# Pairing attention heads anew and sending the first pair's row of maxima of batch 0 by itself

## The chip, the cores and the metric

One Trainium2 chip, one core. The metric is the device time of the kernel in microseconds, the median of several executions.

## The reference, cut to what matters

Eight sequences of 512 token ids pass a token embedding (a row of a table times a 64 x 64 matrix chosen by the token's rule), one attention layer and one mixture-of-experts layer, each behind a layernorm and added to the residual. Only the attention concerns the change:

```python
def _L0_attn_ref(x, Q, K, VO):                        # x (8, 512, 64), Q and K (8, 32, 64), VO (8, 64, 64)
    q = jnp.einsum('btd,hrd->bhtr', x, Q)
    k = jnp.einsum('bud,hrd->bhur', x, K)
    scores = jnp.einsum('bhtr,bhur->bhtu', q, k) / sqrt(d)
    attn = jax.nn.softmax(scores, axis=-1)
    ctx = jnp.einsum('bhtu,bud->bhtd', attn, x)
    return jnp.einsum('bhtd,hde->bte', ctx, VO)
h = _L0_tok_ref(...)
h = h + _L0_attn_ref(_layernorm(h), ...)
h = h + _L0_ffn_ref(_layernorm(h), ...)
```

## The kernel before, in words

**The token stage.** Tokens are scattered into an order by rule in DRAM, in two halves: batches 0 and 1, then batches 2 to 7. Groups of 512 rows are loaded (e_in), transposed on TensorE (turn, L1146, "rT"), copied by ScalarE to eT (L705), multiplied by their rule's matrix (apply, L1155, "rule"), copied by VectorE to y_out (L1022), stored to y_sorted and at last gathered back by GpSimd into hbuf (bring, L551). The first half has 15 groups and is done before the attention begins. The second half has 19 groups. They run as 20 slots in stage 0, in the steps that R_AT gives; a slot is the transposition of one group and the rule of the one before. For them GpSimd issues loads (L413) and stores (L418), and behind the last store the gathers of batches 2 and 3.

**Stages and steps.** From there every engine walks the same loop: a stage b for each batch (from -2), with 16 steps k in each. The order on each engine is written out by hand. In step k of stage b TensorE does: two score tiles for the exponentials, transposed (L1278, keys times queries), one step ahead of their use; up to two score tiles for the maxima of the next batch (s_units, L1303), one before and one after the values; the values (L1319, four matmuls); and what aux_at lists for that step (the lists order, slot and ring give each of these a place in banks 6, 7 and 4). ScalarE takes the exponentials (L684) and copies, VectorE the maxima (L1016), layernorms, the low parts of split numbers and copies. SP's queue is written as one list of DMAs and waits.

**Scores and their maxima.** Queries and keys of a batch come from four projections (proj, L1207 and L1208: two for Q, two for K, four heads of 32 rows in each), split into a high part (qk_h, ScalarE, L753) and a low part (qk_l, VectorE, L1083). stack(b, g) then sends, by DMA, for each row group g of 32 the heads g and 4 + g to three bands of rows of qs and ks: six DMAs of 128 KB a group, 24 a batch (L465 for qs and L468 for ks on SP; for batch 0 the keys' twelve are on ScalarE, L676). Head slots 2g and 2g+1 receive them side by side, so a row of 4 KB stays whole. Each maximum of 128 query rows of a head over its 512 keys is one unit: a matmul and a reduction, 32 a batch. A unit of batch 0 below 16 (first_pair, L1261) reads qk_h and qk_l directly, two heads at a time with three matmuls each, since the stack is still on its way. After 16 units TensorE transposes the maxima ("mt", L1239), ScalarE negates them into negm (L758), and SP sends them as row 96 of qs (max_row, L474), where the exponentials' score tiles pick them up: the matmul of 97 rows subtracts them. Its semaphore is m_in, and the score tiles of head pairs 0 and 1 wait for the first half's row.

**Around the change, before.** The 32 units of batch 0 are in steps (-1, 4) to (0, 3), two a step (LEAD is 12). The transposition mt of its first half is at (-1, 11), behind unit 15. The first two score tiles for the exponentials stand at the head of step (-1, 15), behind unit 21. The rule row of the second half (L1122) follows them. Units 0 to 15 use banks 3 and 4 or 0 and 1 in turn; units 26 to 35 bank 3 alone, as bank 4 serves the rule groups then. The slots are three in step (0, 1), three in (0, 2), eight in (0, 3), three in (0, 4) and three in (0, 5); of a step's slots one stands before the values and the rest behind the other work. xT(1) (L1203) and two projections of batch 1 are in (0, 2), two in (0, 3). The layernorm of batch 1 is in (0, 0) and (0, 1), that of batch 2 begins at (0, 10), that of batch 3 at (0, 15).

Of the kernel before, what the change touches and what calls it, by code (L numbers as in the profile page):

```python
# [24 lines left out]
def packed_weights(Q, K, VO, Wg, bg, gbias, W1, b1, W2, b2):  # L25

    H, R, D = Q.shape
    NE, _, HID = W1.shape
    half = [m.reshape(2, H // 2 * R, D) for m in (Q, K)]
    wqk = np.concatenate([h.transpose(2, 0, 1).reshape(D, -1) for h in half], axis=1)  # L30
    w1 = W1.transpose(1, 0, 2).reshape(D, -1)
    wqk, w1, wg = (np.concatenate([m, m], axis=0) for m in (wqk, w1, Wg))
    vo = np.zeros((2, D, H // 2, 2, D), np.float32)
    row0 = np.zeros((2, D, H // 2, D), np.float32)
    for hh in range(2):
        vo[hh, :, :, hh, :] = VO[hh * (H // 2):(hh + 1) * (H // 2)].transpose(1, 0, 2)
        row0[hh] = VO[hh * (H // 2):(hh + 1) * (H // 2), 0][None]
    w2 = W2.transpose(1, 0, 2).reshape(HID, -1)
    b2p = b2.reshape(NE // 2, 2, D).transpose(1, 2, 0).reshape(2 * D, -1)
    rows = [np.broadcast_to(v[None, :], (128, NE)) for v in (bg, gbias)]  # L40
    stay = [vo.reshape(128, -1), row0.reshape(128, -1), w2, b1.T, b2p, wg] + rows
    return np.ascontiguousarray(np.concatenate(stay + [wqk, w1], axis=1).astype(np.float32))


def lm_tower_kernel(nc, ids_in, table, rules, weights, consts, out, dims):
# [6 lines left out]
    J = T // 128  # L52
# [26 lines left out]
    with ctx:  # L79
# [93 lines left out]
        with ExitStack() as part:  # L173
# [7 lines left out]
            scattered_0 scattered_1 eT_ps eT_ok y_ps y_ok xn_ready xa_ready w_h ones_ok w_ok xT_ps x_hi xs_ready  # L181
            xT2_ps x2_hi xs2_ready proj_ps qk_hi qk_lo ks_one s_ps mx_done mt_ps negm_ready m_in
            st_ps exp_done pv_done ctx_copied srow_in rt_ps rsum_ready vo_ps vo_used h1_ready
# [61 lines left out]

        R_AT = [(0, 1 + g // 3) for g in range(6)] + [(0, 3)] * 8 + [(0, 4 + g // 3) for g in range(6)]

# [9 lines left out]
        def aux_at(b, k):  # L257
# [44 lines left out]
        in_four = max(n for n in range(r0, r1 + 1) if place_of[n] == 4)  # L302
        ONE, TWO = 26, 36

# [16 lines left out]
        def emptied(eng, n):  # L321
# [4 lines left out]
            if kind == "rule":  # L326
                eng.wait_ge(S["y_ok"], b + 1)
            if kind == "mt":
                eng.wait_ge(S["negm_ready"], 2 * b + i + 1)
# [105 lines left out]
        def _(sp):  # L435
# [22 lines left out]
            def stack(b, g):  # L458

                if g == 0:  # L460
                    sp.wait_ge(S["qk_lo"], 4 * b + 4)
                if b >= 2:
                    sp.wait_ge(S["exp_done"], 32 * (b - 2) + 8 * (g + 1))
                for s, src in enumerate((qk_h, qk_l, qk_h)):
                    sp.dma_start(qs[32 * s:32 * s + 32, b % 2, 2 * g:2 * g + 2, :].bitcast(F32),  # L465
                                 src[32 * g:32 * g + 32, 0:2, :].bitcast(F32)).then_inc(S[f"stack_{g}"], 16)
                for s, src in enumerate((qk_h, qk_h, qk_l) if b else ()):
                    sp.dma_start(ks[32 * s:32 * s + 32, b % 2, 2 * g:2 * g + 2, :].bitcast(F32),  # L468
                                 src[32 * g:32 * g + 32, 2:4, :].bitcast(F32)).then_inc(S[f"stack_{g}"], 16)

            def max_row(b, half):

                sp.wait_ge(S["negm_ready"], 2 * b + half + 1)
                sp.dma_start(qs[96:97, b % 2, 4 * half:4 * half + 4, :].rearrange("o h (t n) -> o (h t) n", n=128).bitcast(F32),  # L474
                             negm[:, half, :].bitcast(F32)).then_inc(S["m_in"], 16)
                sp.wait_ge(S["m_in"], 32 * b + 16 * half + 16)
# [6 lines left out]
            for b in range(-2, B):  # L483
# [163 lines left out]
        def _(act):  # L647
# [22 lines left out]
            for b in range(-2, B + 1):  # L670
                for k in range(16):
                    if (b, k) == (-2, PROJ[3] + 1):
                        act.wait_ge(S["qk_lo"], 4)
                        for g in range(4):
                            for s, src in enumerate((qk_h, qk_h, qk_l)):
                                act.dma_start(ks[32 * s:32 * s + 32, 0, 2 * g:2 * g + 2, :].bitcast(F32),  # L676
                                              src[32 * g:32 * g + 32, 2:4, :].bitcast(F32)).then_inc(S[f"stack_{g}"], 16)
# [14 lines left out]
                    for n_, a in enumerate(aux_at(b, k) + [("", 0, 0)]):  # L692
# [61 lines left out]
                        if kind == "mt":  # L754
                            act.wait_ge(S["mt_ps"], 2 * ab + i + 1)
                            if ab >= 1:
# [8 lines left out]
        def _(dve):  # L765
# [224 lines left out]
            for b in range(-2, B + 1):  # L990
# [3 lines left out]
                for k in range(16):  # L994
# [15 lines left out]
                    for nb, u in s_units(b, k):  # L1010
                        n = 32 * nb + u
                        dve.wait_ge(S["s_ps"], n + 1)
                        if nb >= 1 and u % 16 == 0:
                            dve.wait_ge(S["mt_ps"], 2 * nb - 1 + u // 16)
                        at_ = u % 16 if n >= 16 else n % 2 * 8 + n // 2
                        V.tensor_reduce(mx[:, u // 16, at_:at_ + 1], score_bank(n)[:], AX.X, ALU.max).then_inc(S["mx_done"], 1)  # L1016
# [86 lines left out]
        def _(pe):  # L1103
# [82 lines left out]
            def aux(a):  # L1186
# [42 lines left out]
                if kind == "back":  # L1229
# [4 lines left out]
                    for p in range(NE // 2):  # L1234
                        last = nc.tensor.transpose(out_[:, p * 128:(p + 1) * 128], hid_of(f)[:, 2 * p, j * 128:(j + 1) * 128], ident)
                    last.then_inc(S["bk_ps"], 1)
                if kind == "mt":
                    pe.wait_ge(S["mx_done"], 32 * b + 16 * (i + 1))
# [27 lines left out]
            for b in range(-2, B + 1):  # L1266
                for k in range(16):
                    step = 16 * b + k + 1
                    for u in (2 * step, 2 * step + 1):
                        if 0 <= u < 32 * B:  # L1270
                            ub, pair, ut, th = scored(u)
                            pe.wait_ge(S["m_in"], 32 * ub + 16 * (pair // 2 + 1))
                            if u >= NST:
# [14 lines left out]
                    def score_tile():  # L1288
# [9 lines left out]
                        h, tt = u // J, u % J  # L1298
                        pe.wait_ge(S[f"stack_{h // 2}"], 96 * (nb + 1))
                        if n == TWO:  # L1300
# [8 lines left out]
                    if 0 <= b < B:  # L1309
# [58 lines left out]
```

## Time and profile before

| | us |
|---|---|
| median of 3 runs | 592.49 (586.88 to 597.73) |
| the profiled execution's own time | 592.44 |
| its span | 590.4 |
| PE busy | 498.6 (84%) |
| VectorE busy | 417.8 (71%) |
| ScalarE busy | 280.3 (47%) |
| GpSimd busy | 228.2 (39%) |

PE, DVE, ACT, POOL and SP are TensorE, VectorE, ScalarE, GpSimd and SyncE. A timeline has one line for one or several like instructions in a row: start and length in us, engine, line of the kernel, operation, tile written and tiles read, how many, and in brackets how long the engine had stood before and what released it. ACTq and SPq are the issues of DMAs by these engines.

### The profile page before, as it was taken

Reading aid. Unit: us, or ns where it says so; the run is one execution under the profiler, and the core shown is the slowest. Engines: PE = TensorE matmul, PEld = TensorE weight load, DVE = VectorE, ACT = ScalarE, POOL = GpSimd, SP = SyncE. Lnnn points to the kernel's source line nnn. Section 1 sums busy time; section 2 is a strip of 40 time slices with the busy share of each in tenths; the row PEclk is TensorE's granted clock in tenths of the full one; section 3 lists DMA queues with packets and bytes.
Section 4 is the critical chain, followed back from the end, with each engine's and each line's share of the span. In section 5 each row is a group of like instructions: output and inputs, shape, how many; then the busy total and the mean of one; then the engine's idle time right before and its main releaser. Section 6 shows DMA issues by size and latency. Waiting matters only on the chain.

```text
span 590.4 us, 9478 instructions
## 1 busy us (share of the span) xinstructions
PE 498.6 (84%) x2764; PEld 272.0 (46%) x2764; DVE 417.8 (71%) x1008; ACT 280.3 (47%) x562; POOL 228.2 (39%) x375
## 2 busy tenths in 40 slices
PE   0169337876889899999999999999999899999984
PEld 0037314354534344455445534544454455576663
DVE  6644688753376869889698869968865975755477
ACT  0205110245444454565645565555556455556773
POOL 5787376624262002502551253133122513281542
PEclk9997855589897899999999999999999999999988
DMA  8826218426710724404402340422045000000000
GB/s 232 317 81 192 80 26 184 121 73 194 210 45 12 161 56 107 119 2 108 116 5 59 76 100 2 108 64 54 3 107 118 1 2 12 2 11 1 11 2 18
DMA packets 21791, 47.05 MB, mean 80 GB/s; under 512 B 6248, under 2 KB 11576, under 8 KB 21680
## 3 DMA queue, kind: packets, MB, share of 16 engines
q1 hardware_dynamic: 15408, 32.23, 22.3%
q0 software_dynamic: 4752, 8.20, 4.9%
q10 hardware_dynamic: 1584, 6.03, 3.2%
q8 instruction: 25, 0.41, 0.3%
q14 instruction: 22, 0.18, 0.1%
HBM read 9.97 MB, written 11.01 MB: 36 GB/s over the span
## 4 chain that ended last, share of the span: by engine, by line
PE 59%; DVE 19%; issue 7%; POOL 6%; ACT 3%; DMA 3%; SPq 3%; DVEq 0%; ACTq 0%; POOLq 0%
PE bank L1319 14%; PE bank L1303 10%; PE bank L1278 7%; DVE mx L1016 4%; PE bank L1226 4%; PE bank L1248 4%; PE bank L1155 4%; POOL ctxT L535 3%; PE bank L1220 2%; PE bank L1146 2%; PE bank L1221 2%; PE bank L1330 2%; DVE r_sb L1078 1%; SPq L465 1%; POOL emb_sorted L543 1%
## 5 line engine op out<-in xcount | busy, mean ns | idle before, releaser
L1016 DVE TENSOR_REDUCE mx<-bank 128x1 f32<-128x512 f32 x256 | 170.7, 687 | 59.1 <-PE bank L1303 54.5
L604 POOL TENSOR_TENSOR r_sb<-r_sb 128x256 f32<-128x256 f32 x174 | 90.6, 521 | 244.7 <-DVE r_sb L1096 164.1
L684 ACT ACTIVATE prob<-bank 128x512 f32<-128x512 f32 x256 | 138.8, 596 | 71.5 <-PE bank L1278 59.0
L1319 PE MATMUL bank<-prob,xa 128*64 128x512 f32 x448 | 124.1, 633 | 0.0
L1303 PE MATMUL bank<-ks,qs 96*128 96x512 f32 x240 | 112.2, 471 | 12.1 <-DVE mx L1016 12.0
L1303 PEld LDWEIGHTS bank<-ks,qs 96*128 96x128 f32 x240 | 46.5, 195 | 121.4 <-issue 103.9
L1278 PE MATMUL bank<-qs,ks 97*128 97x512 f32 x224 | 78.5, 433 | 0.0
L747 ACT ACTIVATE r_sb<-bank,stay 128x512 f32<-128x512 f32 x56 | 37.1, 687 | 44.8 <-PE bank L1221 44.6
L1278 PEld LDWEIGHTS bank<-qs,ks 97*128 97x128 f32 x224 | 39.5, 198 | 15.4 <-issue 10.5
L1319 PEld LDWEIGHTS bank<-prob,xa 128*64 128x64 f32 x448 | 22.6, 137 | 37.5 <-issue 35.2
L551 POOL DMA_INDIRECT hbuf<-y_sorted,pos x32 | 31.3, 978 | 20.2 <-DMA y_sorted<-y_out 11.5
L535 POOL DMA_INDIRECT ctxT<-in_table,ids x32 | 32.4, 1011 | 13.5 <-issue 9.3
L543 POOL DMA_INDIRECT emb_sorted<-ctxT,pos x32 | 32.4, 1011 | 12.8 <-issue 9.6
L1248 PE MATMUL bank<-stay,ctxT 128*128 128x128 f32 x256 | 33.7, 276 | 0.1
L1248 PEld LDWEIGHTS bank<-stay,ctxT 128*128 128x128 f32 x256 | 32.4, 191 | 2.2 <-ACT negm L758 0.4
L753 ACT CAST qk_h<-bank 128x512 fp32r<-128x512 f32 x32 | 18.4, 588 | 26.8 <-PE bank L1208 24.1
L1220 PE MATMUL bank<-xs,w_h 128*128 128x512 f32 (+1 forms) x72 | 29.8, 419 | 0.0
L1226 PE MATMUL bank<-r_sb,stay 128*64 128x512 f32 x112 | 27.8, 606 | 1.6 <-ACT r_sb L747 1.6
L1155 PE MATMUL bank<-r_sb,eT 128*64 128x64 f32 (+1 forms) x544 | 26.6, 249 | 2.5 <-DVE y_out L1022 0.9
L1083 DVE TENSOR_TENSOR qk_l<-bank,qk_h 128x512 fp32r<-128x512 f32 x32 | 21.7, 688 | 9.9 <-ACT qk_h L753 9.6
L1096 DVE TENSOR_TENSOR r_sb<-bank,rsum 128x512 f32<-128x512 f32 x30 | 20.7, 691 | 10.4 <-PE bank L1248 7.4
L1221 PE MATMUL bank<-xs,w_l 128*128 128x512 f32 (+1 forms) x72 | 27.0, 380 | 0.0
(173 smaller groups left out, 676.1 us busy)
## 6 DMA issues: line engine op xcount, KB each, us to landing
qs<-qk_h SPq DMA_DIRECT2D x64, 128.0 KB, 2.5
ks<-qk_h SPq DMA_DIRECT2D x56, 128.0 KB, 2.5
qs<-qk_l SPq DMA_DIRECT2D x32, 128.0 KB, 2.5
ks<-qk_l SPq DMA_DIRECT2D x28, 128.0 KB, 2.5
emb_sorted<-front ACTq DMA_DIRECT2D x4, 608.0 KB, 10.3
y_sorted<-y_out POOLq DMA_DIRECT2D x19, 128.0 KB, 3.4
e_in<-emb_sorted POOLq DMA_DIRECT2D x9, 256.0 KB, 4.1
emb_sorted<-front ACTq DMA_DIRECT2D x3, 640.0 KB, 9.3
```

The costliest lines, as they stand in the source:

```text
L535: nc.gpsimd.indirect_dma_start(etok[:, c, :], None, table, bass.IndirectOffsetOnAxis(ap=ids[:, 1, c:c + 1], axis=0)).then_inc(e_got[c // Q ...
L604: nc.gpsimd.tensor_tensor(a[:, at:at + width], src[:, 0:width], src[:, width:2 * width], ALU.add).then_inc(S["pool_chain"], 1)
L684: nc.scalar.activation(prob[:, step % NPROB, u % 2, :], bank[u % NST][:], ACT.Exp, scale=SC).then_inc(S["exp_done"], 1)
L1016: V.tensor_reduce(mx[:, u // 16, at_:at_ + 1], score_bank(n)[:], AX.X, ALU.max).then_inc(S["mx_done"], 1)
L1155: last = M(out_[half * TS:(half + 1) * TS, c * D:(c + 1) * D], eT[:, g % 2, col:col + TS], r_sb[:, at_:at_ + D] if isinstance(at_, int) el ...
L1220: M(o, w1_h[:, i * HID:(i + 1) * HID], x2, start=True, stop=False)
L1221: M(o, w1_l[:, i * HID:(i + 1) * HID], x2, start=False, stop=True).then_inc(S["up_ps"], 1)
L1226: last = M(out_[64 * t:64 * t + 64, 0:x2_of(b).shape[1]], w2_f[:, 2 * i + t, :], hid_of(b)[:, 2 * i + t, :], start=True, stop=True)
L1248: last = M(out_[:, pair * 128:(pair + 1) * 128], ctxT[:, b % 2, pair, i * 128:(i + 1) * 128], vo_blk[:, pair, :, :].rearrange("p t e -> p ...
L1278: last = M(bank[u % NST][:], keys[:, h, :], qs[:, ub % 2, h, :], start=True, stop=True)
L1303: M(score_bank(n)[:], qs[0:96, nb % 2, h, tt * 128:(tt + 1) * 128], ks[0:96, nb % 2, h, :], start=True, stop=True).then_inc(S["s_ps"], 1)
L1319: last = M(bank[5][64 * hh:64 * hh + 64, :], xa[:, b % XAR, ut, :], prob[:, step, hh, :], start=(ut == 0), stop=(ut == J - 1))
```

## The change

Heads are paired 0 with 1, 2 with 3 and so on within each projection, so that the first eight units of batch 0 are the whole of head slots 0 and 1. Their maxima get a transposition ("mq"), a copy and a DMA (first_row, semaphore m_q) of their own. Units 0 to 15 of batch 0 move to steps (-1, 8) to (-1, 15), two a step, and units 16 to 31 to steps (0, 0) to (0, 3), four a step. The other half's transposition mt(0, 0) moves to (0, 0). The rule slots move: eight in step (0, 3), four each in (0, 4), (0, 5) and (0, 6). The stretch of units on bank 3 alone becomes 28 to 37, and units 14 and 15 go to banks 3 and 4. Stacking DMAs write slots two apart. Parts of the diff:

```diff
-        vo[hh, :, :, hh, :] = VO[hh * (H // 2):(hh + 1) * (H // 2)].transpose(1, 0, 2)
+        heads = [H // 2 * (p % 2) + 2 * (p // 2) + hh for p in range(H // 2)]
+        vo[hh, :, :, hh, :] = VO[heads].transpose(1, 0, 2)
...
-        R_AT = [(0, 1 + g // 3) for g in range(6)] + [(0, 3)] * 8 + [(0, 4 + g // 3) for g in range(6)]
+        R_AT = [(0, 3)] * 8 + [(0, 4 + g // 4) for g in range(12)]
...
-            if (b, k) == (-1, 11) or k == MT[0] and 0 <= b < B - 1:
+            if (b, k) == (-1, 11):
+                todo.append(("mq", 0, 0))
+            if (b, k) == (0, 0):
+                todo.append(("mt", 0, 0))
+            if k == MT[0] and 0 <= b < B - 1:
                 todo.append(("mt", b + 1, 0))
...
-        ONE, TWO = 26, 36
+        ONE, TWO = 28, 38
...
+        def first_of(g):
+            return 4 * (g // 2) + g % 2
...
         def s_units(b, k):
-            nb, kk = divmod(16 * b + k + LEAD, 16)
+            at_ = 16 * b + k
+            if at_ < 4:
+                u = 2 * (at_ + 8) if at_ < 0 else 16 + 4 * at_
+                return [(0, n) for n in range(u, u + (2 if at_ < 0 else 4))] if u >= 0 else []
+            nb, kk = divmod(at_ + LEAD, 16)
...
-            return bank[(3 if n >= 16 or n // 2 % 2 == 0 else 0) + n % 2]
+            return bank[(3 if n >= 14 or n // 2 % 2 == 0 else 0) + n % 2]
...
-                    sp.wait_ge(S["exp_done"], 32 * (b - 2) + 8 * (g + 1))
+                    sp.wait_ge(S["exp_done"], 32 * (b - 2) + 16 * (g // 2 + 1))
...
-                    sp.dma_start(qs[32 * s:32 * s + 32, b % 2, 2 * g:2 * g + 2, :].bitcast(F32),
+                    sp.dma_start(qs[32 * s:32 * s + 32, b % 2, first_of(g):first_of(g) + 3:2, :].bitcast(F32),
...
+            def first_row():
+                sp.wait_ge(S["negm_q"], 1)
+                sp.dma_start(qs[96:97, 0, 0:2, :].rearrange("o h (t n) -> o (h t) n", n=128).bitcast(F32),
+                             negm[0:2 * J, 0, :].bitcast(F32)).then_inc(S["m_q"], 16)
+                sp.wait_ge(S["m_q"], 16)
...
-                if b in (-1, 0):
-                    max_row(b + 1, 0)
+                if b == -1:
+                    first_row()
+                    max_row(0, 0)
+                if b == 0:
+                    max_row(1, 0)
...
+                        if kind == "mq":
+                            act.wait_ge(S["mq_ps"], 1)
+                            nc.scalar.mul(negm[0:2 * J, 0, :], ring(a)[0:2 * J, 0:128], -1.0).then_inc(S["negm_q"], 1)
...
+                if kind == "mq":
+                    pe.wait_ge(S["mx_done"], 8)
+                    nc.tensor.transpose(out_[0:2 * J, 0:128], mx[:, 0, 0:2 * J], ident).then_inc(S["mq_ps"], 1)
...
-                    pe.wait_ge(S["mx_done"], n - 2)
+                    pe.wait_ge(S["mx_done"], n - 2 if n < 14 else n)
...
-                            pe.wait_ge(S["m_in"], 32 * ub + 16 * (pair // 2 + 1))
+                            if u < 2:
+                                pe.wait_ge(S["mx_done"], 12)
+                            if ub == 0:
+                                for g in (pair // 2 * 2, pair // 2 * 2 + 1):
+                                    pe.wait_ge(S[f"stack_{g}"], 96)
+                            if ub == 0 and pair == 0:
+                                pe.wait_ge(S["m_q"], 16)
+                            else:
+                                pe.wait_ge(S["m_in"], 32 * ub + 16 * (pair // 2 + 1))
...
-                    score_tile()
+                    for _ in range(3):
+                        score_tile()
```

## Rows read from the trace of the kernel before

**Rows 1.** The page, part 2, in 40 slices of 14.76 us

```profile
PE   0169337876889899999999999999999899999984
...
PEclk9997855589897899999999999999999999999988
```

**Rows 2.** Timeline of ScalarE around the first row: start us, us, engine, line, operation

```profile
89.24 1.48 ACTq L676 DMA_DIRECT2D ks<-qk_h  x2
...
102.66 1.64 ACTq L676 DMA_DIRECT2D ks<-qk_l  x1
104.43 0.27 ACT L758 ACTIVATE negm<-bank 16x128 fp32r<-16x128 f32 x1 [15.94 <-PE bank L1239]
```

**Rows 3.** Timeline of SyncE's queue, same stretch

```profile
102.63 1.55 SPq L465 DMA_DIRECT2D qs<-qk_h  x1
104.72 0.88 SPq L474 DMA_DIRECT2D qs<-negm  x1
```

**Rows 4.** Waits on tile qs, 100 to 112 us: releaser, us, times

```profile
  DMA qs<-negm: 0.2, 1
```

**Rows 5.** Timeline of TensorE, stages -1 and 0

```profile
99.65 0.79 PE L1261 MATMUL bank<-qk_h 32*128 32x512 f32 x2 [0.16 <-DVE mx L1016]
...
107.42 1.36 PE L1303 MATMUL bank<-ks,qs 96*128 96x512 f32 x2 [0.28 <-DVE mx L1016]
108.59 1.07 PE L1278 MATMUL bank<-qs,ks 97*128 97x512 f32 x2
...
125.09 0.60 PE L1203 MATMUL bank<-cst,xn 128*128 128x128 f32 x4
...
131.99 1.07 PE L1278 MATMUL bank<-qs,ks 97*128 97x512 f32 x2
...
135.96 0.39 PE L1208 MATMUL bank<-xs,wqk_l 128*128 128x512 f32 x1
136.91 0.41 PE L1146 MATMUL bank<-cst,e_in 128*128 128x128 f32 x2 [0.56 <-DVE y_out L1022]
...
142.62 0.41 PE L1146 MATMUL bank<-cst,e_in 128*128 128x128 f32 x2 [0.47 <-issue]
...
148.84 1.22 PE L1278 MATMUL bank<-qs,ks 97*128 97x512 f32 x2
...
156.40 0.73 PE L1278 MATMUL bank<-qs,ks 97*128 97x512 f32 x2
...
165.72 1.08 PE L1319 MATMUL bank<-prob,xa 128*64 128x512 f32 x4
...
167.87 1.08 PE L1319 MATMUL bank<-prob,xa 128*64 128x512 f32 x4
...
176.05 0.47 PE L1303 MATMUL bank<-ks,qs 96*128 96x512 f32 x1 [1.91 <-DVE mx L1016]
```

**Rows 6.** Timeline of VectorE, stages -1 and 0

```profile
101.30 2.57 DVE L1016 TENSOR_REDUCE mx<-bank 128x1 f32<-128x512 f32 x4 [0.52 <-PE bank L1261]
...
111.69 1.29 DVE L1016 TENSOR_REDUCE mx<-bank 128x1 f32<-128x512 f32 x2 [0.45 <-PE bank L1303]
112.90 0.41 DVE L910 TENSOR_REDUCE ln_s<-hbuf 128x4 f32<-128x256 f32 x1
...
118.72 0.69 DVE L936 TENSOR_TENSOR xn<-ln_c,ln_s 128x512 f32<-128x512 f32 x1
...
172.62 0.42 DVE L910 TENSOR_REDUCE ln_s<-hbuf 128x4 f32<-128x256 f32 x1 [0.37 <-DMA hbuf<-y_sorted,pos]
```

**Rows 7.** Timeline of GpSimd, last store and first gather of the second half

```profile
162.87 1.18 POOL L418 DMA_DIRECT2D y_sorted<-y_out  x2 [0.75 <-DVE y_out L1022]
166.32 1.03 POOL L551 DMA_INDIRECT hbuf<-y_sorted,pos  x1 [2.27 <-DMA y_sorted<-y_out]
```

**Rows 8.** DMA queues, 88 to 109 us, then 42 to 60 us: packets, MB, share

```profile
q10 hardware_dynamic: 576, 1.57, 37.5%
...
q1 hardware_dynamic: 3378, 3.18, 55.0%
```

More of the change, by code:

```diff
@@ L35, in packed_weights @@
     for hh in range(2):
-        vo[hh, :, :, hh, :] = VO[hh * (H // 2):(hh + 1) * (H // 2)].transpose(1, 0, 2)
-        row0[hh] = VO[hh * (H // 2):(hh + 1) * (H // 2), 0][None]
+        heads = [H // 2 * (p % 2) + 2 * (p // 2) + hh for p in range(H // 2)]
+        vo[hh, :, :, hh, :] = VO[heads].transpose(1, 0, 2)
+        row0[hh] = VO[heads, 0][None]
     w2 = W2.transpose(1, 0, 2).reshape(HID, -1)
@@ L181, in lm_tower_kernel @@
             scattered_0 scattered_1 eT_ps eT_ok y_ps y_ok xn_ready xa_ready w_h ones_ok w_ok xT_ps x_hi xs_ready
-            xT2_ps x2_hi xs2_ready proj_ps qk_hi qk_lo ks_one s_ps mx_done mt_ps negm_ready m_in
+            xT2_ps x2_hi xs2_ready proj_ps qk_hi qk_lo ks_one s_ps mx_done mt_ps negm_ready m_in mq_ps negm_q m_q
             st_ps exp_done pv_done ctx_copied srow_in rt_ps rsum_ready vo_ps vo_used h1_ready
@@ L327, in emptied @@
                 eng.wait_ge(S["y_ok"], b + 1)
+            if kind == "mq":
+                eng.wait_ge(S["negm_q"], 1)
             if kind == "mt":
@@ L462, in stack @@
                 if b >= 2:
-                    sp.wait_ge(S["exp_done"], 32 * (b - 2) + 8 * (g + 1))
+                    sp.wait_ge(S["exp_done"], 32 * (b - 2) + 16 * (g // 2 + 1))
                 for s, src in enumerate((qk_h, qk_l, qk_h)):
-                    sp.dma_start(qs[32 * s:32 * s + 32, b % 2, 2 * g:2 * g + 2, :].bitcast(F32),
+                    sp.dma_start(qs[32 * s:32 * s + 32, b % 2, first_of(g):first_of(g) + 3:2, :].bitcast(F32),
                                  src[32 * g:32 * g + 32, 0:2, :].bitcast(F32)).then_inc(S[f"stack_{g}"], 16)
                 for s, src in enumerate((qk_h, qk_h, qk_l) if b else ()):
-                    sp.dma_start(ks[32 * s:32 * s + 32, b % 2, 2 * g:2 * g + 2, :].bitcast(F32),
+                    sp.dma_start(ks[32 * s:32 * s + 32, b % 2, first_of(g):first_of(g) + 3:2, :].bitcast(F32),
                                  src[32 * g:32 * g + 32, 2:4, :].bitcast(F32)).then_inc(S[f"stack_{g}"], 16)
+            def first_row():
[3 more added lines that the diff above has]
+                sp.wait_ge(S["m_q"], 16)
             def max_row(b, half):
                 sp.wait_ge(S["negm_ready"], 2 * b + half + 1)
+                if b == 0 and half == 0:
+                    sp.dma_start(qs[96:97, 0, 2:4, :].rearrange("o h (t n) -> o (h t) n", n=128).bitcast(F32),
+                                 negm[2 * J:4 * J, 0, :].bitcast(F32)).then_inc(S["m_in"], 16)
+                    sp.wait_ge(S["m_in"], 16)
+                    return
                 sp.dma_start(qs[96:97, b % 2, 4 * half:4 * half + 4, :].rearrange("o h (t n) -> o (h t) n", n=128).bitcast(F32),
@@ L675, in _ @@
                             for s, src in enumerate((qk_h, qk_h, qk_l)):
-                                act.dma_start(ks[32 * s:32 * s + 32, 0, 2 * g:2 * g + 2, :].bitcast(F32),
+                                act.dma_start(ks[32 * s:32 * s + 32, 0, first_of(g):first_of(g) + 3:2, :].bitcast(F32),
                                               src[32 * g:32 * g + 32, 2:4, :].bitcast(F32)).then_inc(S[f"stack_{g}"], 16)
@@ L753, in _ @@
                             nc.scalar.copy(qk_h[:, i, :], ring(a)[:]).then_inc(S["qk_hi"], 1)
+                        if kind == "mq":
+                            act.wait_ge(S["mq_ps"], 1)
+                            nc.scalar.mul(negm[0:2 * J, 0, :], ring(a)[0:2 * J, 0:128], -1.0).then_inc(S["negm_q"], 1)
                         if kind == "mt":
+                            if ab == 0 and i == 0:
+                                act.wait_ge(S["m_q"], 16)
                             act.wait_ge(S["mt_ps"], 2 * ab + i + 1)
@@ L1014, in _ @@
                             dve.wait_ge(S["mt_ps"], 2 * nb - 1 + u // 16)
-                        at_ = u % 16 if n >= 16 else n % 2 * 8 + n // 2
+                        at_ = u % 16 if n >= 16 else 8 * (n // 8) + n % 2 * J + n // 2 % J
                         V.tensor_reduce(mx[:, u // 16, at_:at_ + 1], score_bank(n)[:], AX.X, ALU.max).then_inc(S["mx_done"], 1)
@@ L1236, in aux @@
                     last.then_inc(S["bk_ps"], 1)
+                if kind == "mq":
+                    pe.wait_ge(S["mx_done"], 8)
+                    nc.tensor.transpose(out_[0:2 * J, 0:128], mx[:, 0, 0:2 * J], ident).then_inc(S["mq_ps"], 1)
                 if kind == "mt":
@@ L1298, in score_tile @@
                         h, tt = u // J, u % J
-                        pe.wait_ge(S[f"stack_{h // 2}"], 96 * (nb + 1))
+                        pe.wait_ge(S[f"stack_{h // 4 * 2 + h % 2}"], 96 * (nb + 1))
                         if n == TWO:
```

## The prediction

> **What bounds the kernel now.** I read the 40 slices of the page first: from the fifteenth on TensorE is busy in nine tenths of nearly every slice at the full clock, so from there to the end any delay of the start is simply carried through. The hole is in slices 7 to 12 (89 to 177 us), where PE is at 6 to 8 tenths, and slices 6 to 8 show half the clock, 1.2 of 2.4 GHz [rows 1]. The change works in that hole, so I then read the timelines of the engines there, in order of time.
>
> The start of batch 0's exponentials hangs on one small transfer. ScalarE issues twelve stacking DMAs of keys from 89.24 us; the last issue ends at 104.30, and only then can it copy the maxima, at 104.43 [rows 2]. SP issues twelve for the queries over the same time, the last until 104.18, and sends the row of maxima at 104.72 [rows 3]. The first score tile for the exponentials (L1278) starts at 108.59, and the view of the tile's waits says what released it: the row [rows 4, 5]. So the row lands near 108.4, 3.7 us after its issue. The sixteen first-pair maxima are done at 103.9 (101.30 + 2.57) [rows 6].
>
> The next limit is the rule groups of batches 2 and 3 (20 slots, each a transposition and the rule before it). They are interleaved into steps k = 0..5 of stage 0 and end at about 162.8, when the last store is issued; then the gather by POOL from 166.32, and the layernorm of batch 2 at 172.62, which VectorE reaches 0.37 us before its data [rows 6, 7]. PE stands 1.91 us for it (176.05) [rows 5]. So the end of the groups, plus 9.8 us, sets step k = 10 of stage 0, and all later stages shift with it; of the layernorm of batch 3, at k = 15, nothing of the kind is to be feared, as its gathers follow at once.
>
> **The change part by part.**
>
> *The early row.* After 8 of 16 maxima (four come every 3.09 us, 0.52 idle and 2.57 busy, so the eighth is there at 103.87 - 6.18 = 97.7 [rows 6]) a transposition, a copy of 8 rows and a DMA are added. But the copy stands on ScalarE behind the twelve issues that end at 104.30, and the DMA on SP behind the ones that end at 104.18 [rows 2, 3]. It can't be earlier than 104.4, and its row is issued at 104.7 and lands at 108.4, where the row of before lands. Bounds: nothing gained; or, if the issues ended early, 5.6 us (the twelfth maximum is there at 102.3, then 0.14 and a load, about 103.0 against 108.6). I take nothing, since both queues' last issue is in the rows. The added transposition holds PE until 97.9, which delays the next pair by 1.4 us; a pair takes 1.65 us (99.65 to 101.30) [rows 5, 6]. With units 14 and 15 moved into bank 3 and behind the wait, VectorE has 14 maxima at about 104.1 and then nothing to do but tile_rules.
>
> *What is late next.* Before, units 16 to 21 filled the wait for the row, and 22 maxima were done at 109.5. After, PE's queue has the score tile (which waits for the row) ahead of units 14 and 15: 14 maxima stand at 108.6. Then the score tiles 1.07, the rule row 0.6, a pair 1.65: VectorE resumes at 112.0, where before it worked on units 22 and 23 (111.69) [rows 5, 6]. It is 8 maxima (5.2 us at 0.645 each) behind.
>
> *Steps 0 to 2.* From 112.0 VectorE owes 14 maxima (14 to 27), 9.0 us, and the layernorm of batch 1, 112.90 to 119.41 less one pair of 1.29, 5.2 us [rows 6]. That gives 126.3, with 0.8 for single waits 127.1, against 125.09 before for the transposition xT [rows 5]. Then the same 3.3 us to the end of the first two projections (130.4), and step 3 begins at once, where before it began at 131.99, behind groups 4 and 5 [rows 5]. In step 3 units 28 to 31 come four at a time on one bank (ONE is 28), each 0.47 of PE, 0.69 of VectorE and two handovers of 0.14, 1.4 us, two more than before less what ran beside other work: +2.6 over the 4.36 us that step 3 took to the end of its projections at 136.35 (135.96 + 0.39). Sum: 130.4 + 4.4 + 2.6 = 137.4, 1.0 later than before. By then it has one group done where before had seven.
>
> *The groups.* Seven groups follow the projections in step 3 in both kernels: 11.9 us before (136.91 to 148.84); at the pitch of 136.91 to 142.62, four groups in 5.71, 1.43 each, they would be 10.0 [rows 5]. Steps 4 and 5 took 13.9 us (148.84 to 162.8) with six slots. After, steps 4 to 6 hold twelve: six slots more, 8.6 us, and one step more at 2.15 (165.72 to 167.87). The groups end 1.0 + 8.6 + 2.15 = 11.7 us later; the lower price is 1.9 less if the seven keep the best pitch, and 1.7 less again if the half clock that fell into step 4 does not come back (1.22 against 0.73 for the same two score tiles at 148.84 and 156.40). A still lower bound is a pure count of work: eight more units at 0.4, a dearer pair and the added step, with all idle time as before, is +5. Between +5 and +11.7 I take +9, nearer the row analogue, because the moved groups no longer fill VectorE's wait. The gather adds its 9.8 us to whichever end, so k = 10 shifts by the same 9; PE's wait there grows by about 2.2 us, since one step less lies between.
>
> *Halved runs.* A head pair is no longer adjacent in qs and ks, so each partition's 4 KB run becomes two of 2 KB. Row: ScalarE's queue took 37.5% of 16 engines over 21 us, 126 us for 1.57 MB, 80 us per MB; the queue that moved runs of under 1 KB took 55.0% over 18 us for 3.18 MB, 50 us per MB [rows 8]. Small runs were not dearer by the byte, so I take zero; the other end is a doubling of those 15 us. The Trainium skill (DMA: Bandwidth & Descriptors, Why small descriptors are slow (HBM only)) says that transfers inside SBUF are spared that penalty, and gives some 3 cycles per packet beside 32 bytes a cycle; by it the estimate is 134 against 131 cycles per 4 KB, 2%, about 0.3 us over the stack, which would make the time 601.7. No run here shows it yet.
>
> *The rest.* The stacks of batch b+2 now wait for 16 or 32 exponentials instead of 8 to 24; they are issued behind the projections (k = 8) or behind the row of k = 13, when all but the last pair are done, so at most about a microsecond on SP, hidden before the row of sums: 0, at worst 1 in all if that cover goes. Extra score_tile calls find nothing to do. VO's new order of heads is host work. Later banks and waits are the same.
>
> **Sum.** The profiled execution is 592.44 us (span 590.40 and 2.04 around it), level with the median of 592.49. 592.4 + 9 = 601.4.
>
> **Rivals.**
> 1. *Groups denser than taken*: 1.43 throughout, no half clock, +3 to +6, about 597. For it: the first eight groups' inputs are long loaded when they run. Against: before, one store and one load per group beside the stack of batch 1 stretched them too.
> 2. *The row does go early* (the not-slower end): if ACT and SP get their issues away by 98, the row lands near 102, the exponentials start at 103.0, 5.6 us sooner, and VectorE's idle 4 us goes; +9 - 5.6 - 4 gives about -1, some 592, down to 587 if the groups are dense as well. It decides where the last ACT issue ends: before 98.5 the change pays. Against: 104.30.
> 3. *The half clock stays* over steps 0 to 3, as PE has less to do there: each step is then PE's, four units at 0.68 (1.36 for two), the score tiles 1.07 and the values 2.1 (twice the 1.08 of 165.72), 5.9 us against VectorE's 5.2 [rows 5], and 3 us more in step 2: +4, about 605.5. For it: the half clock over slices 6 to 8.
> 4. *The halved runs cost double*: 15 us more before the row lands, 616. Against: rows 8.
>
> **How the numbers follow.** Forecast 0.55 (its own range 598 to 605), rival 1 0.15, rival 2 0.11, rival 3 0.14, rival 4 0.05. Leaving a part of rivals 2 and 4 outside gives 591 to 609. The bound is 2% (580.6 and 604.3), about what a measurement of this kernel can tell from no change, the three runs being 586.88 to 597.73. Slower by over 2%: rivals 3 and 4, and the upper edge of the forecast, 0.27; faster 0.02; within 0.71.
>
> **What would show it.** Right: ACT's last key issue near 104, the early row's issue right behind it near 104.7, the first L1278 near 108.6; VectorE idle for some 4 us between 105 and 112; xT near 127; the last y_sorted store near 172; batch 2's layernorm 9.8 us behind it; from there every step as long as before. Wrong: a first L1278 before 105 (rival 2), a last store before 168 (rival 1), issue rows on ACT twice as long (rival 4), or a layernorm of batch 2 that does not wait for its gather.

## The result and the profile after

The changed kernel took 607.03 us (median of 4 runs, 600.63 to 614.55), the kernel before 589.94 in the same comparison; the ratio is 1.0257 (95% interval 1.0196 to 1.0318). A repetition with 6 runs gave 603.67 us and 1.0248 (1.0207 to 1.0288). The ratios, here and below, leave out every execution more than 1.5% above the fastest of its kernel, so they differ a little from the quotients of the medians. The profiled execution took 600.63 us against the 592.44 of before: 8.2 us, where I had forecast 9. So the time lies in the range and the direction is as forecast. The two ratios stand for 14.6 to 15.2 us, more than the 9.

First the page of the changed kernel: the span, TensorE's busy tenths and clock in 40 slices of 15.0 us, and SP's DMA queue (packets, MB, share of 16 engines).

```profile
span 598.8 us, 9519 instructions
...
PE   0169246776897799999999999999999999999984
...
PEclk9998755589997899999999999999999999999989
...
q1 hardware_dynamic: 21168, 32.23, 21.6%
```

The hole in front is longer than in [rows 1]: slices 7 to 14, to 210 us, have the tenths 6, 7, 7, 6, 8, 9, 7, 7 where the kernel before has 7, 8, 7, 6, 8, 8, 9, 8, and from slice 15 on both have nines. The queue carries its 32.23 MB in 21168 packets instead of 15408, and its share is 21.6% of 598.8 us instead of 22.3% of 590.4, so the halved runs took it no more time.

ScalarE around the early row (start, length, engine, line, operation), then SP's issue of that row:

```profile
102.77 1.80 ACTq L706 DMA_DIRECT2D ks<-qk_l  x1
104.63 0.27 ACT L786 ACTIVATE negm<-bank 8x128 fp32r<-8x128 f32 x1 [16.78 <-issue]
```

```profile
104.92 0.77 SPq L489 DMA_DIRECT2D qs<-negm  x1
```

These answer to [rows 2, 3]. The copy of the eight maxima (L786) waits for nothing that the trace shows ("issue"): it comes when the twelfth issue is done, at 104.63. The row goes at 104.92, where the old one went at 104.72.

TensorE:

```profile
108.42 1.19 PE L1324 MATMUL bank<-qs,ks 97*128 97x512 f32 x2 [6.15 <-DMA qs<-negm]
...
126.71 0.60 PE L1238 MATMUL bank<-cst,xn 128*128 128x128 f32 x4
...
137.36 0.40 PE L1243 MATMUL bank<-xs,wqk_l 128*128 128x512 f32 x1
...
146.21 0.72 PE L1324 MATMUL bank<-qs,ks 97*128 97x512 f32 x2
148.83 0.66 PE L1349 MATMUL bank<-ks,qs 96*128 96x512 f32 x1 [1.90 <-DMA ks<-qk_l]
...
156.92 0.73 PE L1324 MATMUL bank<-qs,ks 97*128 97x512 f32 x2
...
165.12 0.73 PE L1324 MATMUL bank<-qs,ks 97*128 97x512 f32 x2
...
171.19 0.69 PE L1190 MATMUL bank<-r_sb,eT 128*64 x16 [0.40 <-ACT eT L735]
...
185.28 0.77 PE L1349 MATMUL bank<-ks,qs 96*128 96x512 f32 x1 [4.17 <-DVE mx L1051]
```

The first score tiles for the exponentials (L1324, L1278 of before) start at 108.42 against 108.59, and PE stood 6.15 us for the row. The transposition of batch 1's normed rows is at 126.71 (before 125.09), the last projection of step 3 ends at 137.76 (136.35), steps 4, 5 and 6 begin at 146.21, 156.92 and 165.12, and the last rule is applied at 171.9. At 148.83 there is a wait that the old trace lacks, 1.90 us for keys of batch 1. In step 10 PE stands 4.17 us where it stood 1.91 [rows 5].

VectorE, first beside the row, then at the layernorm of batch 2:

```profile
102.28 1.29 DVE L1051 TENSOR_REDUCE mx<-bank 128x1 f32<-128x512 f32 x2 [0.52 <-PE bank L1299]
...
110.17 0.28 DVE L900 CAST trow<-bank 1x128 int32<-1x128 f32 x1 [5.95 <-PE bank L1157]
111.74 1.29 DVE L1051 TENSOR_REDUCE mx<-bank 128x1 f32<-128x512 f32 x2 [1.29 <-PE bank L1299]
```

```profile
181.86 0.42 DVE L945 TENSOR_REDUCE ln_s<-hbuf 128x4 f32<-128x256 f32 x1 [2.63 <-DMA hbuf<-y_sorted,pos]
```

It has 14 maxima at 103.6, does tile_rules, and is then idle for 5.95 and 1.29 us; units 14 and 15 follow at 111.74, where [rows 6] has units 22 and 23 at 111.69. The layernorm starts at 181.86 against 172.62.

All of the loss arises before 250 us. These are the fifth and the last layernorm from 100 us on, first in the kernel before, then in the changed one:

```profile
241.07 0.42 DVE L910 TENSOR_REDUCE ln_s<-hbuf 128x4 f32<-128x256 f32 x1
...
570.75 0.29 DVE L910 TENSOR_REDUCE ln_s<-hbuf 128x2 f32<-128x128 f32 x1
```

```profile
249.04 0.42 DVE L945 TENSOR_REDUCE ln_s<-hbuf 128x4 f32<-128x256 f32 x1
...
578.82 0.29 DVE L945 TENSOR_REDUCE ln_s<-hbuf 128x2 f32<-128x128 f32 x1
```

They are 8.0 and 8.1 us apart, so behind that point the rest of the kernel takes as long as before.

GpSimd, the rule groups' loads, first and last store and the first gather:

```profile
113.17 2.93 POOL L428 DMA_DIRECT2D e_in<-emb_sorted  x4 [1.47 <-DMA emb_sorted<-ctxT,pos]
139.86 0.57 POOL L433 DMA_DIRECT2D y_sorted<-y_out  x1 [23.77 <-DVE y_out L1057]
...
172.64 0.54 POOL L433 DMA_DIRECT2D y_sorted<-y_out  x1 [0.55 <-DVE y_out L1057]
175.42 1.03 POOL L581 DMA_INDIRECT hbuf<-y_sorted,pos  x1 [2.25 <-DMA y_sorted<-y_out]
```

The inputs of the first eight groups are loaded from 113.17 on, but the first store is at 139.86, after 23.77 us with nothing to do. The last store's issue ends at 173.2 (172.64 + 0.54) against 164.1 (162.87 + 1.18 for two) [rows 7]; I name the last store by that end from here on.

### The profile page after: what moved, and what is told of

Read it like the earlier page. It is cut to its first block, busy times and chain, and to the rows that moved or that the text cites. A ratio compares the mean times of both kernels' runs of the same rounds, so it can differ in the third digit from the quotient of the medians.

```text
span 598.8 us, 9519 instructions
## 1 busy us (share of the span) xinstructions
PE 499.9 (83%) x2765; PEld 269.5 (45%) x2765; DVE 417.8 (70%) x1008; ACT 280.3 (47%) x563; POOL 229.0 (38%) x375
## 3 DMA queue, kind: packets, MB, share of 16 engines
q1 hardware_dynamic: 21168, 32.23, 21.6%
## 4 chain that ended last, share of the span: by engine, by line
PE 60%; DVE 16%; POOL 7%; issue 6%; DMA 4%; ACT 3%; ACTq 3%; SPq 1%; DVEq 0%; POOLq 0%
PE bank L1365 16%; PE bank L1349 11%; PE bank L1324 8%; PE bank L1261 5%; PE bank L1286 4%; DVE mx L1051 3%; POOL ctxT L565 3%; ACTq L706 3%; PE bank L1190 2%; PE bank L1255 2%; PE bank L1256 2%; PE bank L1376 2%; DVE r_sb L1113 1%; PE bank L1181 1%; POOL emb_sorted L573 1%
## 5 line engine op out<-in xcount | busy, mean ns | idle before, releaser
L634 POOL TENSOR_TENSOR r_sb<-r_sb 128x256 f32<-128x256 f32 x174 | 90.5, 520 | 243.6 <-DVE r_sb L1131 162.8
L1365 PE MATMUL bank<-prob,xa 128*64 128x512 f32 x448 | 125.8, 641 | 0.0
L1324 PE MATMUL bank<-qs,ks 97*128 97x512 f32 x224 | 79.0, 435 | 6.2 <-DMA qs<-negm 6.2
L777 ACT ACTIVATE r_sb<-bank,stay 128x512 f32<-128x512 f32 x56 | 37.0, 686 | 44.9 <-PE bank L1256 44.7
L1324 PEld LDWEIGHTS bank<-qs,ks 97*128 97x128 f32 x224 | 39.4, 196 | 23.2 <-issue 18.5
L766 ACT ACTIVATE r_sb<-bank,stay 128x512 f32<-128x512 f32 x28 | 19.3, 688 | 16.4 <-PE bank L1261 16.4
L1190 PE MATMUL bank<-r_sb,eT 128*64 128x64 f32 (+1 forms) x544 | 24.6, 236 | 2.5 <-ACT eT L697 1.0
```

The costliest lines, as they stand in the source:

```text
L634: nc.gpsimd.tensor_tensor(a[:, at:at + width], src[:, 0:width], src[:, width:2 * width], ALU.add).then_inc(S["pool_chain"], 1)
L777: nc.scalar.activation(hid_of(ab)[:, i, :], ring(a)[:, 0:x2_of(ab).shape[1]], ACT.Relu, bias=b1_f[:, i:i + 1]).then_inc(S["relu_done"], 1)
L1324: last = M(bank[u % NST][:], keys[:, h, :], qs[:, ub % 2, h, :], start=True, stop=True)
L1365: last = M(bank[5][64 * hh:64 * hh + 64, :], xa[:, b % XAR, ut, :], prob[:, step, hh, :], start=(ut == 0), stop=(ut == J - 1))
```

## Experiments

All ratios are to runs of the kernel before on the same chip in the same comparison.

**Is it the new pairing?**

```diff
-    sp.dma_start(qs[32 * s:32 * s + 32, b % 2, 2 * g:2 * g + 2, :].bitcast(F32),
+    sp.dma_start(qs[32 * s:32 * s + 32, b % 2, first_of(g):first_of(g) + 3:2, :].bitcast(F32),
```

(with the same for ks, VO's order, the order of the maxima, and the stacks' waits for 16 and 32 exponentials; all else as before)

> The kernel before with the new pairing of heads alone: weights, stacking DMAs with slots two apart (4 KB runs cut into two of 2 KB), the later waits of the stacks on the exponentials; no early row, units and rule groups as before. My theory: the pairing costs nothing, 0 to +1 us; twelve key issues on ScalarE still end near 104.3 and the row still lands near 108.4. Rival (halved runs cost): if the new layout is what makes the changed kernel slower, most of its 15 us between the medians stays, some +8 us or more. Rival (later stack waits cost): about +1 us per stage, +4 in all.

Measured: 590.79 us in 10 runs, ratio 1.002 (0.9983 to 1.0057). Neither the halved runs nor the later waits of the stacks cost anything that can be measured; rival 4 is out. The Trainium skill (DMA: Bandwidth & Descriptors, Why small descriptors are slow (HBM only)) says that transfers inside SBUF escape the penalty of small runs, and the run agrees. But this trace shows something else: TensorE's first and last mark of the seven groups in step 3 and GpSimd's last store and first gather.

```profile
135.24 0.41 PE L1151 MATMUL bank<-cst,e_in 128*128 128x128 f32 x2 [0.55 <-DVE y_out L1027]
...
145.17 0.74 PE L1283 MATMUL bank<-qs,ks 97*128 97x512 f32 x2
```

```profile
156.81 1.12 POOL L419 DMA_DIRECT2D y_sorted<-y_out  x2 [0.75 <-DVE y_out L1027]
161.56 1.03 POOL L556 DMA_INDIRECT hbuf<-y_sorted,pos  x1 [3.64 <-DMA y_sorted<-y_out]
```

The seven groups take 9.9 us (135.24 to 145.17) instead of 11.9, and the last store is at 157.9, six us ahead of [rows 7], in a kernel of the same time. A second trace of the kernel before, below, bears on this.

**Does the row come late because it is queued late?**

```diff
-                sp.wait_ge(S["m_q"], 16)
...
+                if b == -1:
+                    first_row()
+                    stack(0, 2)
                 if 0 <= b + 1 < B:
                     stack(b + 1, 3)
...
                 if b == -1:
-                    first_row()
+                    sp.wait_ge(S["m_q"], 16)
                     max_row(0, 0)
...
-                if 0 <= b + 2 < B:
+                if 0 < b + 2 < B:
                     stack(b + 2, 2)
...
-                        for g in range(4):
+                        for g in range(2):
                             for s, src in enumerate((qk_h, qk_h, qk_l)):
                                 act.dma_start(ks[...], ...)
...
                             nc.scalar.mul(negm[0:2 * J, 0, :], ring(a)[0:2 * J, 0:128], -1.0).then_inc(S["negm_q"], 1)
+                            for g in range(2, 4):
+                                for s, src in enumerate((qk_h, qk_h, qk_l)):
+                                    act.dma_start(ks[...], ...)
```

> The changed kernel with the stack of batch 0 split around the early row: ScalarE issues the keys of row groups 0 and 1, copies the eight maxima, then issues groups 2 and 3; SP sends groups 0 and 1, the early row, then 2 and 3. My theory (the row is late only because both queues' twelve issues stand ahead of it): copy near 98, row issued near 98.5, landed by 103, first L1324-kind score tiles near 103 instead of 108.4, exponentials when ScalarE has issued its last six DMAs (105 to 106), VectorE back at its maxima near 107 instead of 111.7; all later steps 4 to 5 us earlier, about 4.5 us less than the changed kernel. Rival (DMA bandwidth, not the order of issue, sets the row's landing): the row lands behind what is in flight, 107 or later, and no more than 1 us is won.

Measured: 599.18 us in 4 runs, ratio 1.0155 (1.0083 to 1.0227), 4.5 us under the repetition of the changed kernel. ScalarE, TensorE and GpSimd's last store:

```profile
97.97 0.27 ACT L788 ACTIVATE negm<-bank 8x128 fp32r<-8x128 f32 x1 [10.31 <-PE bank L1280]
...
103.59 1.08 ACT L716 ACTIVATE prob<-bank 128x512 f32<-128x512 f32 x2 [5.35 <-PE bank L1330]
```

```profile
102.56 1.22 PE L1330 MATMUL bank<-qs,ks 97*128 97x512 f32 x2
...
106.73 1.22 PE L1330 MATMUL bank<-qs,ks 97*128 97x512 f32 x2
```

```profile
169.64 0.54 POOL L433 DMA_DIRECT2D y_sorted<-y_out  x1 [0.54 <-DVE y_out L1063]
```

The copy is at 97.97, the first score tiles start at 102.56, 5.9 us sooner than in the changed kernel. The order of the issues alone had set the row's time. Yet the second pair of score tiles is at 106.73, 4.9 sooner, the last store at 170.2, 3.0 sooner, and the layernorm of batch 2 at 179.87, 2.0 sooner: the early start shrinks on its way, and the kernel stays slower than before. What it wins in time is not sharp. The interval just overlaps that of the repetition (1.0207 to 1.0288), and the profiled executions took 600.72 and 600.63 us at the same mean granted clock of 0.929.

**The rule groups put back, and moved alone**

```diff
-        R_AT = [(0, 3)] * 8 + [(0, 4 + g // 4) for g in range(12)]
+        R_AT = [(0, 1 + g // 3) for g in range(6)] + [(0, 3)] * 8 + [(0, 4 + g // 3) for g in range(6)]
-        ONE, TWO = 28, 38
+        ONE, TWO = 20, 36
```

> The changed kernel with the rule groups back where they were before (three slots in step 1, three in step 2, eight in step 3, three each in 4 and 5; one bank for units 20 to 35). My theory: the groups were not moved into a bad place, the room in steps 1 and 2 is gone; with two banks down to one, units 20 to 31 come at 1.35 us each. Last store near 174, as late as the changed kernel's 173 or up to 3 us later; time within +-3 us of the changed kernel's. Rival (the loss is the six groups moved out of steps 1 and 2 and the step more): last store back near 164, about 8 us less than the changed kernel.

```diff
-        R_AT = [(0, 1 + g // 3) for g in range(6)] + [(0, 3)] * 8 + [(0, 4 + g // 3) for g in range(6)]
+        R_AT = [(0, 3)] * 8 + [(0, 4 + g // 4) for g in range(12)]
-        ONE, TWO = 26, 36
+        ONE, TWO = 30, 38
```

> The kernel before with the changed kernel's places for the rule groups alone (eight in step 3, four each in 4, 5 and 6; one bank for units 30 to 37). My theory: steps 1 and 2 get shorter by the six slots as far as the layernorm lets them, the projections of step 3 end near 130 instead of 136, the last store comes near 165.5 instead of 162.9: +3 us over the kernel before. Rival (moving the groups is the whole loss): +8 us or more. Rival (it costs nothing alone): 0.

Measured: with the groups back in the changed kernel 607.41 us, 1.0328 (1.0235 to 1.0422), no better than the changed kernel and rather worse; with the groups moved alone in the kernel before 596.11 us, 1.0118 (1.0047 to 1.0188). VectorE and the last two stores of the first, then the last store of the second:

```profile
122.28 0.69 DVE L1051 TENSOR_REDUCE mx<-bank 128x1 f32<-128x512 f32 x1 [1.26 <-PE bank L1349]
...
133.49 0.69 DVE L1051 TENSOR_REDUCE mx<-bank 128x1 f32<-128x512 f32 x1 [2.93 <-PE bank L1349]
```

```profile
176.47 1.11 POOL L433 DMA_DIRECT2D y_sorted<-y_out  x2 [0.83 <-DVE y_out L1057]
```

```profile
165.12 0.54 POOL L418 DMA_DIRECT2D y_sorted<-y_out  x1 [0.55 <-DVE y_out L1022]
```

In the first, units 20 to 31 come one by one from a single bank while groups run beside them, with gaps of 0.7 to 2.9 us before a maximum, and the last store falls to 177.6, past the 176 that I had allowed. So the groups' new places are not the loss, and what is left of the change is the early row and the units moved into stage 0. In the changed kernel the new places rather help: the last store is 4.4 us sooner with them and the ratio 1.0248 instead of 1.0328, though these two intervals overlap. By themselves they cost 7 us (1.0118). My number for that was half. By its end the last store is 1.6 us later (165.7 against 164.1), where I had 2.6, and the profiled execution took 594.33 us, 1.9 more, but the ratio stands for 7, not 3.

**The early row with nothing moved**

```diff
-            if at_ < 4:
-                u = 2 * (at_ + 8) if at_ < 0 else 16 + 4 * at_
-                return [(0, n) for n in range(u, u + (2 if at_ < 0 else 4))] if u >= 0 else []
...
-            if (b, k) == (-1, 11):
+            if (b, k) == (-1, 7):
                 todo.append(("mq", 0, 0))
```

(and R_AT, ONE, TWO, the banks and mt(0, 0) as in the kernel before)

> The early row and the new pairing alone: units of batch 0 in the steps of the kernel before (22 of them ahead of the first score tiles), mq behind unit 7, the other half's row behind it, rule groups and banks as before. My theory (the row gains nothing since both queues send it at 104.7; the loss is in what was moved): first score tiles near 108.5 as before, last store within 1 us of the kernel before's, time equal to it within 1 us. Rival (the extra transposition, copy and wait on the first row cost by themselves): +2 us or more.

Measured: 594.76 us in 10 runs, ratio 1.0046 (1.0008 to 1.0083). So the row and the new pairing together cost 0.5%, some 2.7 us by the ratio. That is the rival's value (2 or more) and not mine (within 1), though the interval reaches from 0.5 to 4.9 us and meets that of the pairing alone. In the trace SP issues the first row at 105.73 and the second, which waits until the first has landed, at 108.61; ScalarE's copy for the second waits with it, and the first score tiles come at 109.94. Whether that wait is the cost isn't shown: the second trace of the kernel before, below, has its copy at 105.89 and its first score tiles at 109.67, with no early row at all. Here the last store is at 160.7, not within 1 us of [rows 7], and the fifth layernorm at 238.48. With the groups back in the changed kernel it is at 255.04, and apart from the step of mq these two kernels differ only in the steps, banks and waits of the units and in the step of mt. So the moved units hold the greater part of the loss. Moving them without the early row was not tried.

**The changed kernel again**

> The changed kernel itself again, with more runs, since its profiled execution was 8 us above that of before and its median 15 us or more. Theory A (clock): the steps lose the same 9 us in every execution, and what lies above comes from more time at the half clock; the runs' mean granted clock is 0.915 to 0.93, below the 0.93 to 0.945 of before, and the time falls as it rises; median 600 to 608. Theory B (chance of four runs): median near 599, with clocks as before.

Measured: 603.67 us in 6 runs (601.72 to 606.72), ratio 1.0248 (1.0207 to 1.0288). The mean granted clock was 0.922 to 0.932 of full speed in these runs, 0.917 to 0.929 in the first four, and 0.927 to 0.947 (median 0.937) in 43 runs of the kernel before. Of those that the ratios count, six were at 0.927 to 0.932, with a median of 590.6 us; the four runs of the changed kernel at 0.929 to 0.932 have 601.8. At like clocks the difference is 11 us between medians and 8.2 between the two profiled executions (0.930 and 0.929). The rest, 3 us or more, goes with a lower clock of the changed kernel. The second trace has the steps of the first: last store at 173.5, layernorm of batch 2 at 182.13. So theory A holds in the main: the steps lose 8 to 11 us, where it had 9.

**Six slots each in steps 4 and 5**

```diff
-        R_AT = [(0, 3)] * 8 + [(0, 4 + g // 4) for g in range(12)]
+        R_AT = [(0, 3)] * 8 + [(0, 4 + g // 6) for g in range(12)]
-        ONE, TWO = 28, 38
+        ONE, TWO = 28, 36
```

> The changed kernel with the twelve late rule slots six each in steps 4 and 5 instead of four each in 4 to 6. My theory (the gather behind the last group sets step 10, so each step that runs ahead of the last group costs its 2.15 us): last store 2 us earlier (near 170.5 to 171), all from step 10 on 2 us earlier. Rival (work is only reordered): no change.

Measured: 602.52 us, ratio 1.0206 (1.0165 to 1.0246). TensorE's wait in step 4 and the last store:

```profile
149.87 0.50 PE L1349 MATMUL bank<-ks,qs 96*128 96x512 f32 x1 [1.80 <-DMA ks<-qk_l]
```

```profile
172.41 0.54 POOL L433 DMA_DIRECT2D y_sorted<-y_out  x1 [0.63 <-DVE y_out L1057]
```

A step less ahead of the last group won nothing in the trace: the last store is at 173.0 against 173.2, and the time is the same within the noise. The twelve late groups don't keep 1.43 us plus their steps; something else sets their pace there. In the changed kernel the 16 DMA engines are 91 to 97% busy from 141 to 161 us, with the stack of batch 1 and the loads and stores of the groups, while they moved nothing from 126 to 137 us. But in the kernel before, too, they are 84 to 96% busy from 138 to 156 us. Whether the queues or the groups' own chain set the pace was not tried.

**The kernel before with its groups packed into step 3**

```diff
-        R_AT = [(0, 1 + g // 3) for g in range(6)] + [(0, 3)] * 8 + [(0, 4 + g // 3) for g in range(6)]
+        R_AT = [(0, 1 + g // 3) for g in range(6)] + [(0, 3)] * 14
-        ONE, TWO = 26, 36
+        ONE, TWO = 26, 32
```

> The kernel before with the six rule slots of steps 4 and 5 moved to step 3 (three, three, fourteen). My theory: last store near 157 to 158 instead of 162.9; the gather then ends before step 10 is reached, PE's 1.9 us wait there and perhaps the half clock behind it go; 3 to 4 us faster than the kernel before. Rival (loads, stores and the stack of batch 1 limit the groups' pace, so the exponentials only wait longer): no change or some 2 us slower.

Measured: 590.22 us in 10 runs, ratio 1.0012 (0.9982 to 1.0042). The last store and the layernorm of batch 2:

```profile
156.57 0.54 POOL L418 DMA_DIRECT2D y_sorted<-y_out  x1 [0.51 <-DVE y_out L1022]
```

```profile
169.91 0.41 DVE L910 TENSOR_REDUCE ln_s<-hbuf 128x4 f32<-128x256 f32 x1
```

The store is at 157.1 as expected and the layernorm waits for no gather (no bracket), but my 3 to 4 us are not won: the layernorm starts at 169.9, as in the kernel with the new pairing alone (169.82), since there VectorE is not held by the gather either.

**The kernel before again**

> The kernel before itself, for a second trace. The one shown has its last store at 162.9 us and PE waiting for the gather in step 10; the kernel with the new pairing alone, equal in time, has its last store near 157 and no wait. If the shown trace is a late one among its kind, this trace has the seven groups of step 3 at 1.4 us each (10 us instead of 11.9), its last store between 156 and 160, and VectorE reaching the layernorm of batch 2 after its data. If not, it is at 162 to 163 again and the pairing has moved it.

Measured: one run, 596.48 us. TensorE in step 10 and the last stores:

```profile
174.99 0.47 PE L1303 MATMUL bank<-ks,qs 96*128 96x512 f32 x1 [1.93 <-DVE mx L1016]
```

```profile
161.84 1.12 POOL L418 DMA_DIRECT2D y_sorted<-y_out  x2 [0.74 <-DVE y_out L1022]
```

This trace has the last store at 163.0 and the wait of 1.93 us, like [rows 5, 7]. So the execution shown is not odd in that; yet both traces are of executions above the median of 590 (592.44 and 596.48), and the two traces with the last store at 157 to 158 (new pairing, 589.85 us; groups packed, 587.87 us) are of faster ones. What sets them apart is TensorE's granted clock while the groups run. This is the stretch from 144 to 156 us (its length, PE busy, granted clock, DMA share, GB/s) of [rows 5] and then of the kernel with the new pairing alone:

```profile
144.00:156.00 12.00, 9.18 (x88) 0.72 0.93 262
```

```profile
144.00:156.00 12.00, 10.12 (x127) 1.00 0.88 258
```

It is 0.72 in both traces of the kernel before, and 1.00 with the new pairing alone, with the groups packed and with the early row alone (last store at 160.7). So the late last store goes with a stretch at half clock. Whether the kernel before always falls into it, or only in its slower executions, isn't shown: a trace of it at 588 us is not there. The expectation's first case failed.

**The best arrangement of the change**

```diff
 (on top of the split stack)
-        R_AT = [(0, 3)] * 8 + [(0, 4 + g // 4) for g in range(12)]
+        R_AT = [(0, 2)] * 6 + [(0, 3)] * 8 + [(0, 4 + g // 3) for g in range(6)]
-        ONE, TWO = 28, 38
+        ONE, TWO = 24, 36
```

> The changed kernel with the stack split around the early row (the row lands by 102.5) and six rule slots in step 2, eight in 3, three each in 4 and 5. This is the best arrangement of the change that the runs so far point to. My theory (VectorE's maxima, four a step on one bank, and the groups fill stage 0, so an early start of the exponentials can't be turned into time): last store near 166, 595 to 597 us, still slower than the kernel before. Rival (the row's lateness was the only fault of the change): at or below the kernel before's 590.

Measured: 599.06 us, ratio 1.0148 (1.0103 to 1.0193), the last store at:

```profile
165.80 1.11 POOL L433 DMA_DIRECT2D y_sorted<-y_out  x2 [0.83 <-DVE y_out L1063]
```

With exponentials 6 us early and the last store at 166.9, it is no better than the split alone, above my 595 to 597 us, and 1.5% slower than the kernel before. The last store is only 2.9 us behind that of [rows 7], the layernorm of batch 2 4.5 us (177.07), and the fifth one 6.3 us (247.38), so here most of the loss does not come through the last group. What makes it was not tried. No version with units moved into stage 0 came near the kernel before, and none of all beat it.

## Why the prediction was right

By its own steps:

- *The early row* (nothing gained): right. 104.63, 104.92 and 108.42 against 104.4, 104.7 and 108.4; the split showed that the order of issues is the cause, with 102.56 once it is changed.
- *What is late next*: right. VectorE resumed at 111.74 (forecast 112.0) with 8 maxima owed. Its idle time is 5.95 + 1.29 us, more than the 4 that I had named. With the groups put back the loss stayed, and with the row but no units moved only 2.7 of 15 us were left, so the moved units are its main part.
- *Steps 0 to 3*: 126.71 for the transposition (127.1), 137.76 for the projections (137.4). Right, though by a balance: the transposition came 0.4 sooner than forecast and the first two projections took 4.1 us behind it, not 3.3. PE's granted clock from 108 us to the transposition was 0.63 against 0.78 before, the direction of rival 3.
- *The groups*: the end was right (last store 9.1 us later, forecast 9), the parts were not. The seven groups of step 3 took 8.5 us, not 10 to 11.9. One of their transpositions already stands ahead of the projections. The first six also read their matrices at fixed places, so the kernel loads no registers for them, and the transpositions follow at 1.0 us in this trace (139.90, 140.88, 141.88); in the kernel before all seven of step 3 load registers and follow at 1.3 to 1.5 at best. So step 4 began 2.6 us sooner than before. Step 4 then took 10.7 us, with 1.90 of waiting for batch 1's keys that I had not seen coming, and from its start to the end of the last rule it was 25.7 us against 13.9, 11.8 more where I had 10.75. Two errors of opposite sign and my choice of 9 out of 5 to 11.7 gave the right end, so that is in part luck. The price of a step at 2.15 was not found again in the variant with one step less. My 162.8 for the last store of before is the start of its last two; by the end, as here, it is 164.1.
- *The gather sets step 10*: right for the changed kernel, 9.2 us from that store's start to the layernorm (forecast 9.8), or 8.7 from its end against 8.6 before, and PE's wait grew by 2.3 us (forecast 2.2). For the kernel before it holds in its two traces; in the two variants of the same time with the last store near 157 the layernorm did not wait for the gather.
- *Halved runs* and *the rest*: zero, as taken.
- *The sum*: the terms that were mis-sized are the base and the clock. I made the sum against one execution of 592.44 and took it for the median; 43 runs have 590.0. Between profiled executions the difference is 8.2, at like clocks 11, by the ratios 15. The forecast of 9 fits the first and is too small for the last, as I had given a lower clock no term outside rival 3. The forecast's base was 2.4 us too high, which hid a part of that.

Of the rivals, 1 (denser groups) was half true in step 3 and given back in step 4; 2 was true as to the mechanism, and decided by ScalarE's last issue as said, but worth 4.5 us at most, not 9.6; that VectorE's maxima still had to be done before the groups is my reading of it, not tested by itself; 3 fits the 3 us or more that go with a lower clock, which I did not isolate; 4 is out.

## What to carry to other kernels

Before a result is sent off early, look at what stands in front of it on each queue that it passes: here a copy and a DMA stood behind 24 stacking DMAs, the last of them issued until 104.6 us, and the work that had been moved away to make room for it was just what had filled that wait. Then ask whether the earlier start leads anywhere: with the row 6 us early the last store was only 3 us and the layernorm behind it 2 us sooner. And a single profiled execution can be off the median by several us (596.48 against 590.0 for the kernel before), so compare its clock and time with the runs before building a sum on it.

## What I had not expected

The kernel with a longer hole in front has a lower granted clock over its runs: 0.917 to 0.932, median 0.924, against 0.927 to 0.947, median 0.937. It is 0.909 to 0.918 in the variant whose last store is the latest, which took 607.41 us. Two kernels of equal time (before and with the new pairing alone) have their last group's store at 164.1 and 157.9 us in their traces, and the layernorm waits for the gather in the first and not in the second, so a chain that binds in one trace need not be what sets the time.
